# Two-chunk steps in the masked layer, and another order of TensorE's work in both attention layers

## The reference

```python
x = x + tanh(g_xattn[0]) * L0_xattn(layernorm(x), ctx, ctx, ...)   # 32 score heads of 4, differential attention
x = x + tanh(g_ffn[0]) * L0_ffn(layernorm(x), ...)
x = x + tanh(g_xattn[1]) * L1_xattn(layernorm(x), ctx, ctx, mask, ...)  # 16 heads of 8, masked
x = x + tanh(g_ffn[1]) * L1_ffn(layernorm(x), ...)

# both attentions, per head h
q, k, v = x @ Wq.T, ctx @ Wk.T, ctx @ Wv.T
scores = q_h @ k_h.T * scale            # 56 x 1500; in layer 1 the mask sets some to the lowest float
p = softmax(scores)                     # over the 1500 context tokens
out_h = p @ v_h
```

## Time and profile before

| | |
|---|---|
| median of 3 runs | 2355.09 us (2350.68 to 2356.16) |
| profiled execution | 2361.65 us |
| its span, first to last instruction | 2359.2 us |
| mean granted TensorE clock | 0.946 of full speed |
| busy share of the span | PE 93%, DVE 71%, ACT 64%, POOL 54% |
| layer 0 attention, main loop | about 140 to 1226 us |
| layer 1 attention, main loop | about 1456 to 2180 us |

### The profile page before, as it was taken

The page is one execution under the profiler, slowest core; times in us unless marked ns, Lnnn a source line. Parts: engine busy times, 40 slices in busy tenths (PEclk is TensorE's granted clock), DMA queues, the critical chain, the costliest instruction groups (busy, mean ns, idle before and its releaser), DMA issues. The chain is left out here.

```text
span 2359.2 us, 67435 instructions
## 1 busy us (share of the span) xinstructions
PE 2192.7 (93%) x27256; PEld 1303.0 (55%) x27256; DVE 1677.1 (71%) x3697; ACT 1507.8 (64%) x2133; POOL 1278.9 (54%) x1418
## 2 busy tenths in 40 slices
PE   4799999999999999999967957999999999999798
PEld 3255555555555555555536843666655666666576
DVE  3688888888888888888816555777766677774644
ACT  2177788777877778778763322767666667766322
POOL 5335655655654554655333445777766777762232
PEclk8599999999999999999997975999999999999699
DMA  3635344344444444444201027667665666661100
GB/s 105 128 77 113 96 98 109 101 94 108 106 97 99 112 96 95 115 93 94 48 7 57 24 61 149 137 142 137 143 131 120 127 144 140 138 126 24 54 1 16
DMA packets 113421, 227.82 MB, mean 97 GB/s; under 512 B 46052, under 2 KB 58596, under 8 KB 112612
## 3 DMA queue, kind: packets, MB, share of 16 engines
q1 hardware_dynamic: 113124, 223.67, 42.8%
HBM read 146.77 MB, written 76.48 MB: 95 GB/s over the span
## 5 line engine op out<-in xcount | busy, mean ns | idle before, releaser
L1061 ACT ACTIVATE probs<-score_ps 125x896 f32<-125x896 f32 x1152 | 1014.3, 915 | 210.3 <-PE score_ps L954 207.9
L1119 DVE TENSOR_REDUCE max_part<-max_ps 112x1 f32<-112x500 f32 x1024 | 654.7, 668 | 115.3 <-PE spare_ps L923 68.3
L970 PE MATMUL acc_ps<-probs,vext 125*32 125x224 f32 (+1 forms) x12288 | 673.2, 316 | 6.6 <-issue 6.1
L923 PE MATMUL max_ps<-kstack,qstack 48*112 48x500 f16 x1535 | 508.1, 405 | 4.9 <-DVE max_part L1119 2.6
L954 PE MATMUL score_ps<-qstack,kstack 50*125 50x224 f16 (+1 forms) x6144 | 454.8, 244 | 17.2 <-ACT probs L1061 13.9
L954 PEld LDWEIGHTS score_ps<-qstack,kstack 50*125 50x125 f16 x6144 | 344.4, 134 | 183.8 <-issue 122.2
L1116 DVE CUSTOM_DVE_ANT_0 kstack<-max_ps,kstack 112x500 f32<-112x500 f32 x511 | 335.3, 675 | 134.2 <-PE max_ps L923 80.1
L1119 DVE TENSOR_REDUCE max_part<-spare_ps 112x1 f32<-112x500 f32 x512 | 343.3, 670 | 64.6 <-PE max_ps L923 63.5
L970 PEld LDWEIGHTS acc_ps<-probs,vext 125*32 125x32 f32 x12288 | 261.7, 109 | 225.8 <-issue 156.5
L923 PE MATMUL spare_ps<-kstack,qstack 48*112 48x500 f16 x769 | 310.7, 404 | 20.2 <-issue 16.9
L923 PEld LDWEIGHTS max_ps<-kstack,qstack 48*112 48x112 f16 x1535 | 173.5, 129 | 143.4 <-issue 77.7
(11 more groups left out here) (200 smaller groups left out, 2697.8 us busy)
## 6 DMA issues: line engine op xcount, KB each, us to landing
kstack<-k_parts SPq DMA_DIRECT2D x384, 187.5 KB, 6.6
k_parts<-khl SPq DMA_DIRECT2D x128, 375.0 KB, 2.8
ctx_f<-in_ctx SPq DMA_DIRECT2D x32, 750.0 KB
ctx_f<-context_parts SPq DMA_DIRECT2D x32, 750.0 KB, 4.4
context_parts<-ctx_f SPq DMA_DIRECT2D x16, 750.0 KB, 3.8
context_parts<-kstack SPq DMA_DIRECT2D x16, 750.0 KB, 3.5
mask_in<-in_mask SPq DMA_DIRECT2D x128, 82.0 KB
qrows<-q_parts SPq DMA_DIRECT2D x384, 7.0 KB, 7.0
```

The costliest lines, as they stand in the source:

```text
L923: nc.tensor.matmul(room(("P", n, p))[0:PIECE, 0:TK], qstack[n % SLOTS][rows, c, PIECE * i:PIECE * (i + 1)], kstack[n % SLOTS][rows, c, TK ...
L970: last = nc.tensor.matmul(acc_ps[32 * j:32 * j + 32, TT * S * i:TT * S * (i + 1)].rearrange("p (s c) -> p s c", s=S), vext[n % SLOTS][:, t ...
L1061: nc.scalar.activation(probs[t % 2][:, 896 * h:896 * h + 896].rearrange("k (b c) -> k b c", b=2), score_ps[(t * H + h) % 2][0:KT, :, 0:448 ...
L1119: nc.vector.reduce_max(best, scores, AX.X).then_inc(s_red, 1)
```

## The change

Layer 1 gets 6 steps of two chunks instead of 12 of one (`L.steps`), each chunk in its own half of the score banks, so that both layers have two scores and two exponentials to a step. The product is no longer cut in two: `weigh` issues all its matmuls in a row. Preparations of layer 1 move from the rooms of the search into the score banks, as layer 0 had it, and the output is turned in one use instead of two. `order_of` chooses among four orders of the work in a step, by whether this step and the one before it have preparations. In layer 1 the search of batch `n + 2` begins in step 3 of 6. On the sync queue the context load of layer 1 stands behind the maxima's rows; on GpSimd the two mask conversions change places; the mask load waits for both of them.

```diff
-        self.uses_f = 2
+        self.uses_f = self.halves
+        self.steps = NKT if self.halves == 2 else NKT // 2
...
-        where = {("T", 0): (1, 1), ("F", 0): (2, 1), ("T", 1): (3, 1), ("F", 1): (4, 1), ("T", 2): (5, 1), ("K", 0): (6, 1),
-                 ("M", 0): (7, 1), ("V", 0): (7, 1), ("K", 1): (8, 1), ("V", 1): (9, 1), ("K", 2): (10, 1), ("A", 0): (11, 1),
-                 ("V", 2): (11, 1)}
+        where = {("T", 0): (1, 0), ("F", 0): (2, 0), ("T", 1): (3, 0), ("F", 1): (4, 0), ("T", 2): (5, 0), ("K", 0): (6, 0),
+                 ("M", 0): (7, 1), ("V", 0): (7, 0), ("K", 1): (8, 0), ("V", 1): (9, 0), ("K", 2): (10, 0), ("A", 0): (11, 1),
+                 ("V", 2): (11, 0)}
...
-        where = {("V", 0): (0, 2), ("F", 0): (1, 2), ("V", 1): (2, 2), ("F", 1): (3, 2), ("V", 2): (4, 2), ("K", 0): (5, 2),
-                 ("K", 1): (6, 2), ("M", 0): (7, 2), ("K", 2): (8, 2), ("A", 0): (10, 2)}
+        where = {("F", 0): (1, 1), ("V", 0): (1, 0), ("V", 1): (2, 0), ("V", 2): (2, 1), ("M", 0): (3, 1), ("K", 0): (3, 0),
+                 ("K", 1): (4, 0), ("K", 2): (4, 1), ("A", 0): (5, 1)}
...
-    AHEAD = 5
+    AHEAD = 3 if L.masked else 5
     early = AHEAD * per_step
+    ORDERS = {"both scores first": ("scores 0", "scores 1", "pair 0", "weigh", "pair 1", "prepare"),
+              "scores apart by a pair": ("scores 0", "pair 0", "scores 1", "weigh", "pair 1", "prepare"),
+              "scores apart by the product": ("scores 0", "pair 0", "weigh", "scores 1", "pair 1", "prepare"),
+              "pairs apart by preparation": ("scores 0", "weigh", "scores 1", "pair 0", "prepare", "pair 1")}
+
+    def order_of(n, t):
+
+        busy = [any(kind not in "AM" for kind, _, _ in at_step(*place)) for place in ((n, t), (n, t - 1) if t else (n - 1, STEPS - 1))]
+        if not busy[1]:
+            return ORDERS["both scores first"]
+        if L.masked and not busy[0]:
+            return ORDERS["scores apart by a pair"]
+        return ORDERS["pairs apart by preparation" if L.masked and busy[0] else "pairs apart by preparation" if busy[0] else "scores apart by the product"]
...
             def next_mask(n):
                 if L.masked:
                     sp.wait_ge(s_add, n)
+                    sp.wait_ge(s_big, n)
                     load_mask(sp, T, L, n)
...
                     next_mask(n + 3)
-                    if L.masked:
-                        next_context(n + 4)
...
                 if n + 1 < B:
                     fill_m(n + 1)
                 if n + 3 < B:
+                    if L.masked:
+                        next_context(n + 4)
                     store_k(n + 3)
...
-                if L.masked:
-                    at_least(pe, s_exp, number - 1)
-                elif place == 0:
+                if place == 0:
                     at_least(pe, s_exp, number)
                 else:
                     at_least(pe, s_exp, number - 2)
                     for user in in_scores:
                         if in_scores[user] == step - 1:
                             pe.wait_ge(*drained(user))
...
-                buf = score_ps[(t * H + h) % 2]
-                keys = slice(KT * t, KT * t + KT)
+                buf = score_ps[h]
+                chunk, columns = (t, range(h * 2, h * 2 + 2)) if H == 2 else (2 * t + h, range(PAIRS))
+                keys = slice(KT * chunk, KT * chunk + KT)
...
-            def weigh(n, t, i):
...
+            def weigh(n, t):
+
+                pe.wait_ge(s_exp, (n * STEPS + t + 1) * 2)
+                if t == 0:
+                    at_least(pe, s_os, n)
+                    pe.wait_ge(s_v, NTHIRD * (n + 1))
+                chunks = [(t, 0)] if H == 2 else [(2 * t + h, 896 * h) for h in range(2)]
+                for chunk, column in chunks:
+                    for i in range(2):
+                        for j in range(4):
...
```

## The result

The changed kernel takes 2391.45 us (median; 2377.86 to 2395.19), the kernel before 2355.39 (2350.68 to 2356.16): ratio 1.0147, 95% interval 1.0105 to 1.0189. It is slower, where 2330 was forecast. The profiled execution of after took 2392.21 us with a span of 2390.4 (before: 2361.65 and 2359.2), with a mean granted clock of 0.930 instead of 0.946.

What follows compares the result with a forecast made beforehand. TensorE's queue bound both layers; after the change the key fill would bind layer 1. Layer 0 -41 us, layer 1 +14, its last batches -2, disturbances +5 gave 2338 profiled, 2331 median, said as 2330; range 2270 to 2385.

Steps and rivals of the forecast that it cites:

- layer 0's first step: Start of a layer 0 batch: second scores behind the whole product, 0.61 us more; the second step gains 0.5.
- value steps: Layer 0's three steps preparing values: 0.14 from the joined product plus 0.13 from the pair, a gain of 0.27 us each.
- the context load in layer 1: Sync queue, layer 1: moving this load behind the maxima's rows costs nothing, since its data is needed a batch later.
- four with transpositions or output: Layer 0's four steps with preparations shorter than keys: limited by 1.15 us from pair to pair, gaining 0.1 together.
- key steps: Layer 0's three steps preparing keys: 2.79 us instead of 2.99, a gain of 0.20 each.
- the 1.15 us from pair to pair: Layer 0: least distance between pairs, as VectorE starts reading 0.41 us after the matmul's start and takes 0.68.
- TensorE alone 20.9: Layer 1: batch period by TensorE's own work alone, 20.9 us (20.3 to 21.4).
- the loop without the clock: Layer 1: first pair through last key cast (8.4), store to fill (2.75), fill (11.3) and 0.1: 22.55 us.
- the clock: Layer 1: idle ahead of step 3 drops TensorE to half speed, about +2.0 us in half the batches: +0.9, period 23.45.
- the second rival: Layer 1: clock falls every batch and key store queues behind context load (+0.8); loop 25.35 us, median 2381; chance 0.20.

Runs made afterwards that it cites:

- Run 1: Changed kernel, but layer 0's first step of a batch issues both score products ahead of its product: 2364.24 us, ratio 1.0047 to the kernel before.
- run 2: Changed kernel, but layer 0's first step takes the order scores, product, scores, pair, pair: 2381.93 us, ratio 1.0132 to the kernel before.
- run 10: Changed kernel with layer 0's first-step scores together, layer 1 values and keys earlier, maxima drained before the second pair, context load back ahead of maxima's rows: 2278.23 us.
- run 12: Changed kernel with layer 0's first-step scores together, maxima drained before the second pair, context load ahead of maxima's rows; layer 1 preparation left in place: 2335.34 us.
- run 8: Changed kernel with layer 0's first-step scores together, layer 1 values and keys prepared earlier, maxima drained before the second pair: 2347.89 us, ratio 0.9969.
- run 3: Changed kernel plus eight unused matmuls of 500 columns ahead of step 3's first pair in layer 1: 2377.27 us, ratio 1.0096 to the kernel before.
- Run 9: Changed kernel with layer 1's context load moved back ahead of the maxima's rows on SP's queue: 2361.88 us, ratio 1.0027 to the kernel before.
- run 11: Kernel before with only layer 1's context load moved, to between the maxima's rows and the key store: 2377.39 us, ratio 1.0114.
- run 4: Changed kernel with layer 1's keys prepared in steps 1 and 2, values in 3 and 4, context load behind the key store: 2356.74 us, ratio 1.0013.
- run 6: Changed kernel with layer 1's values prepared in steps 0, 0, 1 and keys in 2, 2, 3: 2404.31 us, ratio 1.0233 to the kernel before.
- run 5: Changed kernel with only layer 1's context load put behind the key store: 2421.87 us, ratio 1.0275 to the kernel before.

## Why the prediction was wrong

The forecast's profiled execution was 2338 and 2392.2 was measured, 54 us more. Layer 0 missed by 28 x (34.83 - 33.6) = 34, layer 1 by 28 x (24.16 - 23.45) = 20. The medians are 61 apart (2330 and 2391): the profiled execution of before stood 6.6 above its median, that of after 0.8, and the last us is rounding. Three terms failed: layer 0's first step, its value steps, and the context load in layer 1, which was put at nothing.

For layer 0 I took each of the twelve steps from its first scores to those of the next, as medians over 29 batches. They add up to 35.00 before and 34.58 after:

| steps of layer 0 | before | after | change | forecast |
|---|---|---|---|---|
| first and second | 5.43 | 6.15 | +0.72 | +0.1 |
| four with transpositions or output | 11.24 | 11.11 | -0.13 | -0.1 |
| three with keys | 8.97 | 8.38 | -0.59 | -0.6 |
| three with values | 9.36 | 8.94 | -0.42 | -0.8 |

- **Layer 0, key steps: right.** 0.59 together, 0.60 forecast.
- **Layer 0, first and second step: failed.** The prediction had "the two of them: +0.6 and -0.5". The first costs 1.37 more than before (3.59 against 2.22), the second gains 0.65 (2.56 against 3.21): +0.7 instead of +0.1, 28 x 0.6 = 17 us. I used the 1.15 us from pair to pair inside a step, and not across the border from the step before, where the last pair now stands directly ahead: 608.42 + 1.15 = 609.57, and the matmul starts at 609.61. So "at 0.25 + 0.31 + 0.89 = 1.45" for the second scores should have been 2.17. Run 1 takes this away and gives 33.99.
- **Layer 0, value steps: half of the forecast gain.** The three gained 0.42, not 0.8, which is 28 x 0.4 = 11 us. The prediction gave each 0.14 for the joined product and 0.13 for the pair. But in a value step the product now starts 0.39 behind the first scores (605.71 to 606.10) where 0.29 was put down, and the last pair takes 0.26 (608.42 to 608.68) instead of 0.21. Why the product starts later there was not tried. These 0.4 are about what run 1 leaves over: 33.95 in undisturbed batches against 33.6.
- **Layer 0, longer batches.** The other 0.25 of the mean (7 us) are single longer batches: four falls of the clock, each 3.4 us at the lower level and each in a batch of 36.1 to 36.2, and one batch of 35.3. No term had them. Runs 1, 2, 10 and 12 have no such fall in the 28 intervals of layer 0, but run 8, with the first step mended, has one of 6.8 us; the wait of the first step is thus not the only cause, and the rest stays open.
- **Layer 1, TensorE alone 20.9: right.** 20.89 in run 3 less its added matmuls, 20.88 in run 10's undisturbed batches.
- **Layer 1, the loop without the clock: right in its terms.** The store is out 0.35 + 7.9 = 8.3 after the pair (forecast 8.4), store to fill is 2.8 in the kernel before (2.75), the fill takes 11.4 (11.3). The four of the 24 batches without a fall ahead of the keys take 23.0 in the mean, with a store to fill of 3.6.
- **Layer 1, the clock: right in size, not in how.** It falls ahead of the keys in 20 of 24 batches, not half, and costs the store 0.9 us in the mean (8.8 against 7.9), not 2.0 in each. Forecast and measurement are both 0.9, which is luck. The rule of the Trainium skill (TensorE: Matmul & The Clock Gate, "Why this matters for your kernels"), which has only longer idles cost the clock, isn't borne out here: the lower clock stood behind idles from 1.4 us on.
- **Layer 1, "the moved context load costs nothing in the forecast": failed.** Store to fill was to be 2.75 and is 3.63, +0.88, which is 28 x 0.88 = 25 us. Period 24.3 in the table less 0.9 of this is the forecast 23.45. Run 9 takes back 0.55 of it and 0.69 of the period, and run 11 shows the same load holding the same store in the kernel before. The other 0.3 are open in part: stores during which a packet of instructions was moved too landed later in every kernel where the load was out of the way (run 9: 3.3 us in 14 batches against 2.6 in ten; run 10: 3.8 against 2.7). I had asked when the load's data was needed, and left the store behind it to the second rival. That rival had the right mechanism and size (+0.8), but with 2.0 for the clock in each batch went on to a period of 25.35; its total of 2381 is nearest to what was measured.

What holds the store is to be seen in the records of single DMA packets. In run 11 the load goes out 0.6 us ahead of the store in the mean. Its packets (6000 bytes each) end 4.4 us behind the store's issue, and the store's own first packet (3000 bytes) starts 3.5 behind it, against 0.9 in the kernel before. So the store's data itself waits for the load's. In the changed kernel, with the load 2.7 us ahead, the first packet starts after 0.9 as before, but the load's last packets still end 1.35 behind the store's issue, and the landing comes 0.8 later than before. The Trainium skill (DMA: Bandwidth & Descriptors, "Queues, rings and completion order") says that a transfer's semaphore increment lands only after every earlier write from that DMA engine. Nothing here contradicts it, but in run 11 most of the delay stands ahead of the store's first packet, and no run tells the rule apart from data that waits in the queue.

One more cause of long batches is in the traces. In runs 4, 6 and 8 TensorE stands eight or nine times in layer 1 ahead of a product with "issue" as the cause (10.2, 6.4 and 9.1 us in all, the longest 2.6), in run 10 four times for 1.5 us:

```profile
PE acc_ps L979 <- issue: 10.2, 9, 2.6
```
```profile
q8 instruction: 210, 3.44, 0.7%
```

The first row is run 4's. The second is of the DMA queues in the kernel before: packets, MB, share. Queue 8 moves 210 packets of 16 KB that the profile calls "instruction", one in some 11 us. Over all fourteen traces, TensorE stands 58 times for 0.6 us or more in layer 1 with "issue" as the cause, and in all 58 such a packet had ended 1.2 to 2.0 us before TensorE went on; by chance it would be one in 14. So these are very probably waits for TensorE's own program. No run changed anything to test it. The four idles of the kernel before from which the prediction took the price of the clock are of this kind, and belong to the disturbed batches by which its mean, 22.96, is above the 22.32 of the others.

## What to carry to other kernels

A large load that is moved can cost what stands behind it on its queue, however late its own data is needed: look at the two transfers behind the new place and at how long they take to be seen as landed. A loop through several engines must be right in all its links at once; an edit that looks useless or harmful alone (run 6, +13 us) can be the largest gain once the next links are free (-57 us between runs 12 and 10), so read after each edit which instruction the queue was waiting on. And a least distance between two instructions holds across the border of a step as well as inside it.

## What was not expected of the hardware

TensorE's granted clock fell to 0.50, the lower of its two levels, 21 times in layer 1 of the changed kernel, during or right behind idles of 1.4 to 3.3 us, for 3.4 us mostly and 6.8 five times: 89 us in 28 batches. One idle of 2.4 us and the ones of 0.8 to 1.4 us were not followed by it. Filling the idle with unused matmuls (run 3) left 31 us, with a median 14 us lower; removing the idle (run 10) left none. The six transfers of a fill, 1.1 MB (6 x 187.5 KB), take 11.3 to 11.6 us from the first issue to the last landing in every kernel whose fill doesn't follow the context load, about 100 KB per us, and 12.3 and 12.6 where it does (runs 4 and 5).
